# Attention and routed experts on one core: another order of work at the program's start and where the experts begin

## The chip, the cores and the metric

The kernel runs on one core of one Trainium2 chip. The metric is the device time of one execution in microseconds (us). Lower is better.

## The reference, cut to what matters

64 sequences of 128 tokens with 256 features go through cross attention with 16 heads, and then through a routed feed-forward layer of 8 experts of which each token takes two. All numbers are 32-bit floats.

```python
x = x + xattn(layernorm(x), ctx, ctx, Wq, bq, Wk, bk, Wv, bv, Wo, bo)
# Q = q @ Wq + bq, K = k @ Wk + bk, V = v @ Wv + bv, 16 heads of 16
# softmax(Q K^T / 4) V, then @ Wo + bo
x = x + ffn(layernorm(x), router, gating, up, down)
# probs = softmax(x @ router); top 2, their probs through a softmax again
# per chosen expert e: (silu(x @ gating[e]) * (x @ up[e])) @ down[e], weighted sum
```

## The kernel before

Each engine has a program of its own, written out by hand in one order, and the engines meet at semaphores: PE (TensorE) is the block from line 484, ACT (ScalarE) from 804, DVE (VectorE) from 990, POOL (GpSimd) from 380, and SP (SyncE) from 263, which issues most DMAs. No scheduler changes the order, so an instruction that waits holds everything behind it on its engine.

**The attention stage.** `run_stage_a` walks over 16 groups of 4 sequences. For sequence i, PE multiplies the first scores (`scores`, L551), the values of the next sequence (`values`), the attention product of the previous one (`attend`, L576) and a transpose of the row maxima (`swap_max`, L557), then a key or query product for the next group (`keys`, `queries`, 128x512 each), and the scores again with the maximum taken off (`scores_swapped`, L565). DVE takes the row maxima (`row_maxes`, L1028), and turns and divides the attention rows (`turn_att` L1041, `divide_by_sums`, `turn_attn` L1056). ACT makes the exponentials in three instructions, of one, one and two banks (`softmax_exp`, L867), and copies products out of the banks (`copy_piece` L855, `copy_values` L861, `copy_normed` L834). The heads of one sequence reach their places in `heads` through DMAs (`spread`, L286): two for keys, two for queries, each from the copied `kT` or `qT`. The program's start, ahead of the first sequence, is written out on its own: loads, the first layernorm, keys, queries and values of group 0. In it `bv` is multiplied by `Wo` on PE, DVE adds the product to `bo_sb`, and POOL needs that for `x_bo` (L427).

**The expert stage.** The chosen rows lie sorted by expert in DRAM (`sorted_x`), written by POOL with indirect DMAs (`write_rows`, L434). A unit is 256 rows of one expert. SP loads it (`load_unit`), DVE turns it (`turn_unit`, L1327) and reads its row weights (`read_rows_ends`), ACT copies the expert's matrices to `held` (`hold`, L878 and L879), PE makes `gate` and `up_` (16 records each in the trace) and `down_`, ACT the silu (L873), DVE the product (`fuse`, L1333). Unit n's `gate` comes ahead of unit n-1's `down_`. What is left of the last two groups, their residual, layernorm and routing, is put between the first units by `behind_tile(t)`, where t is twice the unit's number or one more.

**The seam.** Between the two stages PE has this order, with nothing of the experts ahead of the last `attend`:

```python
pe.wait_ge(s_n2Tc, (GROUPS - 1) * 2)
attend(last, att)
gate(0, 0, 2)
up_(0, 0, 2)
behind_tile(0)      # project(62)
behind_tile(1)      # project(63)
```

`gate` of unit 0 writes banks 0 and 1 and `up_` banks 2 and 3. The four are the banks from which the exponentials of sequence 63 are read. `held[1]` is the same memory as `probs`, and `xs` is the same as `xn`.

## Time and profile before

| | us |
|---|---|
| median of three runs | 1276.99 |
| the three runs | 1276.99, 1273.31, 1278.37 |
| the profiled execution, its own time | 1274.27 |
| its span, first to last instruction | 1272.5 |
| PE busy | 1221.5 |
| DVE, ACT, POOL busy | 645.8, 561.3, 424.4 |
| attention stage, to the last `scores_swapped` | to 533.1 |
| expert stage, from `gate` of unit 0 | from 539.5 |

Times in a timeline are from the span's start. PE is the engine's matmuls, PEld its weight loads. SPq, ACTq and POOLq are DMA issues and other work of those engines' sequencers. A timeline's row merges neighbouring instructions of one kind; its bracket is the engine's idle time before it and what ended that, by the trace's semaphore events. A 32-bit matmul is two records of PE, a transpose one.

### The profile page before, as it was taken

The numbers are of one execution on the slowest core, as the hardware profiler recorded it, in microseconds if no ns is written. First come the engines' busy times: TensorE is split into PE (matmuls) and PEld (weight loads), VectorE is DVE, ScalarE is ACT, GpSimd is POOL, SyncE is SP. The second block draws the span as 40 slices with busy tenths as digits, with TensorE's granted clock in tenths as the row PEclk, the third lists the DMA queues.
The fourth block names the chain that finished last, engine by engine and source line by source line (L and its number), as shares of the span: only waits on it lengthen the run. The fifth ranks groups of instructions, "written<-read, shape, count | busy, mean of one in ns | idle before, by whom it ended". The sixth has DMA issues, their size and how long they took to land.

```text
span 1272.5 us, 30742 instructions
## 1 busy us (share of the span) xinstructions
PE 1221.5 (96%) x11214; PEld 991.1 (78%) x11215; DVE 645.8 (51%) x1762; ACT 561.3 (44%) x924; POOL 424.4 (33%) x354
## 2 busy tenths in 40 slices
PE   6999999999999999799999999999999999999996
PEld 3677777777767676578887888888888888888996
DVE  3778888888888778623453222332222222232332
ACT  3566666666666665535322222222222322222442
POOL 3211333333333333322464222223332322222322
PEclk9999999999999999899999999999999999999999
DMA  4444455545545332424344333333333433333332
GB/s 130 138 117 122 152 152 149 157 151 154 155 140 151 114 117 82 106 48 67 77 89 71 50 50 50 53 52 53 50 50 50 54 50 52 51 50 43 53 51 33
DMA packets 171586, 112.44 MB, mean 88 GB/s; under 512 B 103345, under 2 KB 158641, under 8 KB 171473
## 3 DMA queue, kind: packets, MB, share of 16 engines
q1 hardware_dynamic: 143984, 72.75, 23.2%
q0 software_dynamic: 26400, 37.09, 16.6%
q8 instruction: 76, 1.25, 0.4%
q10 hardware_dynamic: 1088, 1.05, 0.3%
q14 instruction: 38, 0.30, 0.1%
HBM read 48.59 MB, written 45.46 MB: 74 GB/s over the span
## 4 chain that ended last, share of the span: by engine, by line
PE 89%; DVE 4%; DMA 2%; issue 2%; ACT 1%; SPq 0%; POOL 0%; another core or an unknown queue 0%; ACTq 0%; POOLq 0%; DVEq 0%
PE banks L522 71%; PE banks L551 5%; PE banks L565 4%; PE banks L576 4%; DVE row_max L1028 1%; PE banks L528 1%; PE banks L557 1%; DMA heads<-qT 1%; PE banks L592 1%; DMA out<-x_sb,token 1%; PE banks L600 1%; DVE att_rows L1041 1%; DVE q_less L1035 1%; DMA ctxT_sb<-in_ctx 0%; PE banks L606 0%
## 5 line engine op out<-in xcount | busy, mean ns | idle before, releaser
L481 POOL DMA_INDIRECT out<-x_sb,token x135 | 210.4, 1559 | 478.2 <-DVE x_sb L1346 413.5
L873 ACT ACTIVATE qT<-banks 128x1024 f32<-128x1024 f32 (+1 forms) x75 | 70.4, 939 | 488.6 <-PE banks L522 430.4
L1333 DVE TENSOR_TENSOR heads<-qT,banks 128x1024 f32<-128x1024 f32 (+1 forms) x75 | 83.5, 1113 | 356.7 <-PE banks L522 338.8
L522 PE MATMUL banks<-xnT,probs 128*128 128x256 f32 (+1 forms) x1184 | 242.7, 361 | 4.4 <-issue 4.4
L522 PE MATMUL banks<-down_sb,heads 128*128 x1080 | 245.5, 379 | 1.2 <-DVE x_sb L1346 0.9
L522 PE MATMUL banks<-xnT,kT 128*128 128x256 f32 (+1 forms) x1216 | 244.8, 359 | 0.0
L522 PEld LDWEIGHTS banks<-xnT,probs 128*128 128x128 f32 x1184 | 208.6, 191 | 32.9 <-issue 7.9
L522 PEld LDWEIGHTS banks<-xnT,kT 128*128 128x128 f32 x1216 | 213.1, 192 | 26.6 <-issue 1.0
L522 PEld LDWEIGHTS banks<-down_sb,heads 128*128 128x128 f32 x1080 | 204.0, 190 | 29.2 <-issue 2.2
L434 POOL DMA_INDIRECT sorted_x<-xn,slots_now x128 | 125.2, 978 | 251.5 <-PE banks L551 139.6
L1028 DVE TENSOR_REDUCE row_max<-banks 128x16 f32<-128x2048 f32 x64 | 146.6, 2291 | 64.2 <-PE banks L551 64.1
L867 ACT ACTIVATE probs<-banks 128x512 f32<-128x512 f32 (+1 forms) x192 | 128.1, 740 | 41.8 <-PE banks L565 40.5
L1346 DVE TENSOR_SCALAR x_sb<-banks,weight 128x256 f32<-128x256 f32 x135 | 59.8, 480 | 124.1 <-PE banks L522 115.7
L551 PE MATMUL banks<-heads 32*128 32x128 f32 x2048 | 75.0, 283 | 6.7 <-DMA heads<-qT 4.8
L576 PEld LDWEIGHTS banks<-probs,v_aug 128*32 128x32 f32 x2048 | 52.7, 110 | 31.9 <-issue 31.3
L565 PE MATMUL banks<-q_less,heads 32*128 32x128 f32 x2048 | 76.0, 285 | 1.1 <-DVE q_less L1035 1.1
L551 PEld LDWEIGHTS banks<-heads 32*128 32x128 f32 x2048 | 65.3, 189 | 12.9 <-issue 8.8
L576 PE MATMUL banks<-probs,v_aug 128*32 128x128 f32 x2048 | 70.0, 278 | 4.5 <-ACT probs L867 4.5
L522 PE MATMUL banks<-wo_sb,attnT 128*128 128x256 f32 x256 | 73.2, 409 | 0.7 <-DVE attnT L1056 0.7
L565 PEld LDWEIGHTS banks<-q_less,heads 32*128 32x128 f32 x2048 | 63.7, 188 | 11.7 <-issue 9.7
L522 PE MATMUL banks<-ctxT_sb,wk_sb 128*128 128x512 f32 x128 | 61.9, 608 | 8.3 <-DMA ctxT_sb<-in_ctx 7.8
L522 PE MATMUL banks<-wv_sb,ctxT_sb 128*128 128x256 f32 x256 | 66.0, 380 | 0.4 <-ACT probs L867 0.4
(165 smaller groups left out, 1269.2 us busy)
## 6 DMA issues: line engine op xcount, KB each, us to landing
xn<-sorted_x SPq DMA_DIRECT2D x240, 64.0 KB
x_sb<-in_x SPq DMA_DIRECT2D x16, 512.0 KB, 4.0
ctxT_sb<-in_ctx SPq DMA_DIRECT2D x16, 512.0 KB
heads<-kT SPq DMA_DIRECT2D x128, 64.0 KB
heads<-qT SPq DMA_DIRECT2D x128, 64.0 KB
out<-x SPq DMA_DIRECT2D x16, 512.0 KB
gate_sb<-_L_ffn_kernel_gating_EDF SPq DMA_DIRECT2D x8, 512.0 KB
up_sb<-in_L_ffn_kernel_up_EDF SPq DMA_DIRECT2D x8, 512.0 KB
```

Of the source, the lines that this page charges most:

```text
L434: pool.indirect_dma_start(out=sorted_x[:, :], out_offset=bass.IndirectOffsetOnAxis(ap=slots_now[:, g % 2, i:i + 1], axis=0), in_=xn2[:, g ...
L481: pool.indirect_dma_start(out=out[:, :], out_offset=bass.IndirectOffsetOnAxis(ap=token[:, v, h:h + 1], axis=0), in_=ys[:, 2 * u + h, :], i ...
L522: last = nc.tensor.matmul(dst, lhsT, rhs, start=(i == 0), stop=(i == len(pairs) - 1))
L528: last = nc.tensor.transpose(bank[:, b * P:(b + 1) * P], xn[:, b, c * P:(c + 1) * P], ident[:])
L551: last = nc.tensor.matmul(score_banks(i)[:, j, c * TOK:(c + 1) * TOK], q_heads[strip(j), i % 2, c, :], k_heads[strip(j), i % 2, c, :], sta ...
L565: last = nc.tensor.matmul(score_banks(i)[:, j, c * TOK:(c + 1) * TOK], k_heads[strip(j), i % 2, c, :], q_less[strip(j), c, :], start=True, ...
L576: last = nc.tensor.matmul(bank[32 * j:32 * j + 32, q * TOK:(q + 1) * TOK], v_aug[:, i % 3, 4 * q + j, :], probs[:, j, c, :], start=True, s ...
L867: nc.scalar.activation(probs[:, j:j + n].rearrange("p j h t -> p j (h t)"), score_banks(i)[:, j:j + n], ACT.Exp, scale=DK ** -0.5).then_in ...
L873: nc.scalar.activation(gatedT[:, 0:w * F], gate_up[:, 0:w * F], ACT.Silu).then_inc(s_silu, 1)
L1028: nc.vector.reduce_max(row_max[:].rearrange("p (j r a) -> p j r a", r=16, a=2)[:, :, 0:4, 1], score_banks(i).rearrange("p j (h t) -> p j h ...
L1333: nc.vector.tensor_tensor(fusedT[:, u, 0:w * F], gatedT[:, 0:w * F], gate_up[:, 1024:1024 + w * F], ALU.mult).then_inc(s_fuse, 1)
L1346: last = nc.vector.tensor_scalar(ys[:, 2 * u + h, :], work[:, 0, h * D:(h + 1) * D], weight[:, v, h:h + 1], None, ALU.mult)
```

## The change

Six things are done, in the program's start and at the seam.

1. PE multiplies `ident` by itself 12 times into bank 6, ahead of the first keys.
2. `wo` and `wv` are loaded only once x has landed, the second context block once the first has.
3. The queries of group 0 are made in halves: of sequences 0 and 1 first (two products of 128x256, counted on two semaphores of their own), ahead of the product of `bv` with `Wo`, and of sequences 2 and 3 behind it, in banks that the keys have left. ACT copies the second half of the keys behind the two halves of the normed x instead of ahead of them. SP's `spread` of the first two sequences' queries waits for their two copies alone.
4. The first `scores` no longer waits for the copies of all queries and of the values; PE waits for those behind it.
5. At the seam `gate` of unit 0 stands ahead of the last `attend` and waits for the first two exponentials of sequence 63 alone; `project(62)` comes ahead of `up_`. DVE turns unit 0 and reads its weights ahead of `row_maxes(63)`; ACT does `hold(0, 0)` ahead of the square of x1 of sequence 61.
6. ACT copies the logits of group 14 behind unit 1 instead of behind `silu(2)`, and the second half of group 15's x1 ahead of `silu(5)` instead of behind it.

```diff
--- before.py
+++ after.py
@@ -203,6 +203,7 @@
...
         s_piece, s_piece_c = sem("keys_queries_product"), sem("keys_queries_ready")
+        s_first_q, s_first_qc = sem("first_two_queries_product"), sem("first_two_queries_ready")
         s_v, s_vc = sem("values_product"), sem("values_ready")
@@ -280,7 +281,10 @@
...
                 u, b = i // GROUP % 2, i % GROUP
-                wait(sp, s_piece_c, i // GROUP * 4 + 2 + 2 * o)
+                if o == 1 and i < 2:
+                    sp.wait_ge(s_first_qc, 2)
+                else:
+                    wait(sp, s_piece_c, i // GROUP * 4 + 2 + 2 * o)
                 wait(sp, s_scoreT, i - 1)
@@ -302,6 +306,7 @@
...
             sp.dma_start(bo_sb[:], bo.partition_broadcast(P)).then_inc(s_bo, 16)
+            sp.wait_ge(s_ctx[0], 16)
             load_ctx(1, 1)
@@ -623,8 +628,9 @@
...
                     wait(pe, s_x1, i - 2)
-                    wait(pe, s_vc, i + 1)
-                    wait(pe, s_piece_c, min(4 + i, SEQS))
+                    if i > 0:
+                        wait(pe, s_vc, i + 1)
+                        wait(pe, s_piece_c, min(4 + i, SEQS))
                     wait(pe, s_turn, i - 1)
@@ -648,6 +654,9 @@
...
                     wait(pe, s_exp, i * 3 - 1)
+                    if i == 0:
+                        pe.wait_ge(s_piece_c, 4)
+                        pe.wait_ge(s_vc, 1)
                     if b < 3:
@@ -693,19 +702,30 @@
...
             pe.wait_ge(s_masks, 1)
+            for _ in range(12):
+                nc.tensor.matmul(banks[:, 6, 0:P], ident[:], ident[:], start=True, stop=True)
             pe.wait_ge(s_wk, 16)
...
             norm_swapped(0, 1, work[:, 1, :])
+            def front_queries(m, half, bank, signal):
+                pe.wait_ge(s_xt1c, 2)
+                product(bank[:, 0:2 * TOK], [(wq_sb[:, c, m * P:(m + 1) * P], xnT[:, c, half * 2 * TOK:(half + 1) * 2 * TOK])
+                                             for c in range(DC)]).then_inc(signal, 1)
+
+            pe.wait_ge(s_wq, 16)
+            front_queries(0, 0, score[:, 2, :], s_first_q)
+            front_queries(1, 0, score[:, 3, :], s_first_q)
             pe.wait_ge(s_wo, 16)
...
             product(work[:, 0, 0:D], [(bv_rep[:, c, :], wo_sb[:, c, :]) for c in range(DC)]).then_inc(s_bvo, 1)
-            pe.wait_ge(s_wq, 16)
-            queries(0, 0, score[:, 2, :])
-            queries(0, 1, score[:, 3, :])
+            pe.wait_ge(s_piece_c, 2)
+            front_queries(0, 1, score[:, 0, :], s_piece)
+            front_queries(1, 1, score[:, 1, :], s_piece)
             pe.wait_ge(s_wv, 16)
-            values(0, 0, work[:, 1, :])
+            pe.wait_ge(s_first_qc, 1)
+            values(0, 0, score[:, 2, :])
             pe.wait_ge(s_const, 13)
@@ -774,10 +794,12 @@
...
             pe.wait_ge(s_n2Tc, (GROUPS - 1) * 2)
+            wait(pe, s_exp, SEQS * 3 - 1)
+            gate(0, 0, 2)
+            wait(pe, s_exp, SEQS * 3)
             attend(last, att)
-            gate(0, 0, 2)
+            behind_tile(0)
             up_(0, 0, 2)
-            behind_tile(0)
             behind_tile(1)
@@ -896,15 +918,15 @@
...
                         square_x1(i - 3)
-                    if two and b != 2:
-                        square_x1(i - 2)
-                    if b == 2 and prev:
-                        second_norm(g - 1, (2, 3))
                     if i == SEQS - 1:
...
                         hold(0, 0)
+                    if two and b != 2:
+                        square_x1(i - 2)
+                    if b == 2 and prev:
+                        second_norm(g - 1, (2, 3))
                     if nxt and b < 3:
@@ -924,18 +946,31 @@
...
 
-            for w_sb, w, signal in ((wk_sb, wk, s_wk), (wq_sb, wq, s_wq), (wo_sb, wo, s_wo), (wv_sb, wv, s_wv)):
+            def load_matrix(w_sb, w, signal):
                 act.dma_start(w_sb[:], w.rearrange("(c p) n -> p c n", p=P)).then_inc(signal, 16)
+
+            load_matrix(wk_sb, wk, s_wk)
+            load_matrix(wq_sb, wq, s_wq)
+            act.wait_ge(s_x, 16)
+            load_matrix(wo_sb, wo, s_wo)
+            load_matrix(wv_sb, wv, s_wv)
             first_norm(0, (0, 1, 2, 3))
...
             copy_piece(0, 0, 0, score[:, 0, :])
-            copy_piece(0, 0, 1, score[:, 1, :])
             copy_normed(0, 0, banks[:, 7])
             copy_normed(0, 1, work[:, 1, :])
-            copy_piece(0, 0, 2, score[:, 2, :])
-            copy_piece(0, 0, 3, score[:, 3, :])
+            copy_piece(0, 0, 1, score[:, 1, :])
+            def copy_front_queries(m, half, bank, ready, n, signal):
+                act.wait_ge(ready, n)
+                nc.scalar.activation(qT[:, 0, 2 * half:2 * half + 2, m, :], bank[:, 0:2 * TOK].rearrange("p (b t) -> p b t", t=TOK),
+                                     ACT.Identity, bias=bq_sb[:, m:m + 1]).then_inc(signal, 1)
+
+            copy_front_queries(0, 0, score[:, 2, :], s_first_q, 1, s_first_qc)
+            copy_front_queries(1, 0, score[:, 3, :], s_first_q, 2, s_first_qc)
+            copy_front_queries(0, 1, score[:, 0, :], s_piece, 3, s_piece_c)
+            copy_front_queries(1, 1, score[:, 1, :], s_piece, 4, s_piece_c)
             act.wait_ge(s_masks, 3)
-            copy_values(0, work[:, 1, :])
+            copy_values(0, score[:, 2, :])
             run_stage_a(stage_a)
@@ -943,7 +978,7 @@
...
                     square_x1(SEQS - 1)
-                if t == 4:
+                if t == 3:
                     copy_logitsT(GROUPS - 2, att)
@@ -951,8 +986,9 @@
...
                     gap_exp(GROUPS - 2)
-                if t in (9, 10):
-                    copy_x1T(GROUPS - 1, t - 9, work[:, 1, :])
+                if t == 9:
+                    copy_x1T(GROUPS - 1, 0, work[:, 1, :])
+                    copy_x1T(GROUPS - 1, 1, work[:, 1, :])
                 if t == 11:
@@ -1242,6 +1278,18 @@
...
 
+            def turn_unit(n, u, w, loads):
+                dve.wait_ge(s_xs[u], loads * 80)
+                nc.vector.transpose(xsT[:, u, 0:w * D], xs[:, u, 0:w * D].rearrange(
+                    "p (i c r) -> p c i r", i=w * STRIPS, c=DC)).then_inc(s_xtc, 1)
+
+            def read_rows_ends(n, u, v, w):
+                nc.vector.scalar_tensor_tensor(pair[:, 0:w], ends[:, u, 0:w, 2:4], tile_rank[:, bass.ds(n, 1)],
+                                               ends[:, u, 0:w, 0:2], ALU.is_equal, ALU.mult).then_inc(s_pair, 1)
+                nc.vector.tensor_copy(token[:, v, 0:w], ends[:, u, 0:w, 4])
+                dve.wait_ge(s_pair, n + 1)
+                nc.vector.reduce_sum(weight[:, v, 0:w], pair[:, 0:w], AX.X).then_inc(s_meta, 1)
+
             def stage_a(g, u, core, prev, prev2, prev3, nxt, far):
@@ -1252,6 +1300,10 @@
...
                         second_shift(g - 1)
+                    if i == SEQS - 1:
+                        dve.wait_ge(s_piece, GROUPS * 4)
+                        turn_unit(0, 0, 2, 1)
+                        read_rows_ends(0, 0, 0, 2)
                     row_maxes(i)
@@ -1322,23 +1374,11 @@
...
 
-            def turn_unit(n, u, w, loads):
-                dve.wait_ge(s_xs[u], loads * 80)
-                nc.vector.transpose(xsT[:, u, 0:w * D], xs[:, u, 0:w * D].rearrange(
-                    "p (i c r) -> p c i r", i=w * STRIPS, c=DC)).then_inc(s_xtc, 1)
-
             def fuse(n, u, w):
...
                                         ALU.mult).then_inc(s_fuse, 1)
-
-            def read_rows_ends(n, u, v, w):
-                nc.vector.scalar_tensor_tensor(pair[:, 0:w], ends[:, u, 0:w, 2:4], tile_rank[:, bass.ds(n, 1)],
-                                               ends[:, u, 0:w, 0:2], ALU.is_equal, ALU.mult).then_inc(s_pair, 1)
-                nc.vector.tensor_copy(token[:, v, 0:w], ends[:, u, 0:w, 4])
-                dve.wait_ge(s_pair, n + 1)
-                nc.vector.reduce_sum(weight[:, v, 0:w], pair[:, 0:w], AX.X).then_inc(s_meta, 1)
 
@@ -1386,9 +1426,6 @@
...
 
-            dve.wait_ge(s_piece, GROUPS * 4)
-            turn_unit(0, 0, 2, 1)
-            read_rows_ends(0, 0, 0, 2)
             turn_unit(1, 1, 2, 1)
```

PE's order from its first instruction to the first `scores` (`heads`), before and now; `wk_sb`, `wq_sb`, `wo_sb`, `wv_sb` are the four matrices, `att_rows` holds `bv` repeated. Rows that only continue the one ahead are left out.

```order
L522 MATMUL banks<-ctxT_sb,wk_sb 128x512 [waits ctx_loaded_0,wk_loaded,masks_ready]
L528 MATMUL banks<-ident,xn 128x128 [waits x_normed]
L522 MATMUL banks<-wo_sb,att_rows 128x256 [waits bv_repeated,wo_loaded]
L522 MATMUL banks<-xnT,wq_sb 128x512 [waits normedT_ready,wq_loaded]
L522 MATMUL banks<-wv_sb,ctxT_sb 128x256 [waits wv_loaded]
L551 MATMUL banks<-heads 128x128 [waits values_ready,keys_queries_ready,normedT_ready,key_heads_spread_0,bias_out_ready,query_heads_spread_0,masks_ready,consts_ready]
```

```order
L706 MATMUL banks<-ident 128x128 [waits masks_ready]
L706 MATMUL banks<-ident 128x128 x11
L527 MATMUL banks<-ctxT_sb,wk_sb 128x512 [waits ctx_loaded_0,wk_loaded]
L533 MATMUL banks<-ident,xn 128x128 [waits x_normed]
L527 MATMUL banks<-xnT,wq_sb 128x256 [waits normedT_ready,wq_loaded]
L527 MATMUL banks<-wo_sb,att_rows 128x256 [waits bv_repeated,wo_loaded]
L527 MATMUL banks<-xnT,wq_sb 128x256 [waits normedT_ready,keys_queries_ready]
L527 MATMUL banks<-wv_sb,ctxT_sb 128x256 [waits first_two_queries_ready,wv_loaded]
L556 MATMUL banks<-heads 128x128 [waits normedT_ready,key_heads_spread_0,bias_out_ready,query_heads_spread_0,masks_ready,consts_ready]
```

The product for the output bias moved behind the first half of the queries, and the first scores lost two waits.

PE's order at the seam, before and now; `xnT` is the turned unit, `kT` its expert's matrices, `probs` with `v_aug` the last attention product, `attnT` the projections of sequences 62 and 63.

```order
L565 MATMUL banks<-q_less,heads 128x128 x7
L576 MATMUL banks<-probs,v_aug 32x128 [waits probs_ready,values_ready,x1T_ready,att_turned,table_steps,experts_loaded]
L522 MATMUL banks<-xnT,kT 128x256 [waits weights_held,tileT_ready]
L522 MATMUL banks<-xnT,kT 128x256 [waits weights_held]
L522 MATMUL banks<-wo_sb,attnT 128x256 [waits attnT_ready]
L522 MATMUL banks<-wo_sb,attnT 128x256 [waits attnT_ready,att_turned]
```

```order
L570 MATMUL banks<-q_less,heads 128x128 x7
L527 MATMUL banks<-xnT,kT 128x256 [waits probs_ready,tileT_ready,x1T_ready,weights_held,table_steps,experts_loaded]
L581 MATMUL banks<-probs,v_aug 32x128 [waits values_ready,att_turned,probs_ready]
L527 MATMUL banks<-wo_sb,attnT 128x256 [waits attnT_ready]
L527 MATMUL banks<-xnT,kT 128x256 [waits weights_held]
L527 MATMUL banks<-wo_sb,attnT 128x256 [waits attnT_ready,att_turned]
```

The gate moved ahead of the last attention product, and the projection of sequence 62 moved between that and `up_`.

## Rows read from the trace of the kernel before

**Rows 1.** The page: chain that ended last, share of the span by engine.

```profile
PE 89%; DVE 4%; DMA 2%; issue 2%; ACT 1%; SPq 0%; POOL 0%; another core or an unknown queue 0%; ACTq 0%; POOLq 0%; DVEq 0%
```

**Rows 2.** PE's waits from 500 us on: total us, times, longest.

```profile
PE banks L576 <- ACT probs L867: 4.5, 1, 4.5
...
PE banks L600 <- ACT xn2T L838: 1.7, 1, 1.7
...
PE banks L606 <- ACT logitsT L842: 1.3, 1, 1.3
```

**Rows 3.** Timeline of the start: start us, us, engine, line, operation, count, idle before.

```profile
2.79 0.29 POOL L388 TENSOR_SCALAR_AFFINE_SELECT ident<-ident 128x128 f32<-128x128 f32 x1 [0.24 <-POOL v_aug L386]
...
7.80 5.33 PE L522 MATMUL banks<-ctxT_sb,wk_sb 128*128 128x512 f32 x8 [7.80 <-DMA ctxT_sb<-in_ctx]
...
9.34 2.08 ACT L810 ACTIVATE xn<-x_sb,shift,rstd 128x256 f32<-128x256 f32 x4 [4.74 <-DVE shift L1015]
...
12.97 1.04 PE L528 MATMUL banks<-ident,xn 128*128 128x128 f32 x8
```

**Rows 4.** The same timeline, from the copies to the first scores.

```profile
13.76 1.07 ACT L834 ACTIVATE xnT<-banks 128x512 f32<-128x512 f32 x2
...
13.96 2.44 SPq L286 DMA_DIRECT2D heads<-kT  x4
...
14.98 3.67 PE L522 MATMUL banks<-xnT,wq_sb 128*128 128x512 f32 x8
...
15.48 2.35 POOL L427 TENSOR_TENSOR x_bo<-x_sb,bo_sb 128x1024 f32<-128x1024 f32 x1 [6.38 <-DVE bo_sb L1320]
...
18.49 1.03 PE L522 MATMUL banks<-wv_sb,ctxT_sb 128*128 128x256 f32 x4
...
18.69 0.69 ACT L855 ACTIVATE qT<-banks,bq_sb 128x512 f32<-128x512 f32 x1 [1.03 <-PE banks L522]
19.40 2.38 SPq L286 DMA_DIRECT2D heads<-qT  x4
...
22.07 1.17 PE L551 MATMUL banks<-heads 32*128 32x128 f32 x32 [2.56 <-DMA heads<-qT]
```

**Rows 5.** Timeline of the seam, up to the last attention product.

```profile
527.85 2.29 DVE L1028 TENSOR_REDUCE row_max<-banks 128x16 f32<-128x2048 f32 x1 [1.30 <-PE banks L551]
...
531.96 1.17 PE L565 MATMUL banks<-q_less,heads 32*128 32x128 f32 x32
...
533.09 0.67 DVE L1327 STREAM_TRANSPOSE xnT<-xn 128x512 f32<-128x512 f32 x1
...
535.26 2.00 ACT L867 ACTIVATE probs<-banks 128x512 f32<-128x512 f32 x3 [1.31 <-remote]
...
537.62 1.93 PE L576 MATMUL banks<-probs,v_aug 128*32 128x128 f32 x32 [4.49 <-ACT probs L867]
```

**Rows 6.** Timeline of the seam, behind it.

```profile
539.48 9.21 PE L522 MATMUL banks<-xnT,kT 128*128 128x256 f32 x32
...
544.25 0.72 DVE L1041 STREAM_TRANSPOSE att_rows<-banks 128x512 f32<-128x512 f32 x1 [8.24 <-remote]
...
550.25 1.10 PE L522 MATMUL banks<-wo_sb,attnT 128*128 128x256 f32 x4 [0.70 <-DVE attnT L1056]
...
551.19 7.07 PE L522 MATMUL banks<-xnT,probs 128*128 128x256 f32 x32
```

**Rows 7.** POOL's timeline at the seam: first and last of 8 writes in a row.

```profile
537.11 0.97 POOL L434 DMA_INDIRECT sorted_x<-xn,slots_now  x1 [2.74 <-issue]
...
546.00 0.96 POOL L434 DMA_INDIRECT sorted_x<-xn,slots_now  x1 [0.31 <-issue]
```

**Rows 8.** Stretches: length; PE, PEld, DVE, ACT, POOL busy; granted clock; DMA share; GB/s.

```profile
536.80:543.60 6.80, 5.98 (x42) 4.82 (x43) 0.00 (x0) 1.74 (x2) 4.96 (x6) 0.50 0.63 143
...
663.90:673.30 9.40, 6.00 (x23) 3.90 (x22) 1.54 (x4) 0.89 (x1) 6.87 (x8) 1.00 0.40 117
673.30:676.80 3.50, 3.35 (x7) 2.03 (x7) 1.88 (x6) 1.83 (x2) 0.31 (x1) 0.51 0.39 91
```

## The prediction

> **What bounds the kernel now.** I read the page first: the chain of work that ended last is 89% PE [rows 1]. So a change counts only where PE waits or runs slowly, and the next view is the list of PE's waits, which also shows how few there are. From 500 us on three of them concern this change: 4.5 us ahead of the last attention product, 1.7 and 1.3 us for two of ACT's copies [rows 2]. The third view is the timeline of the start. PE's first work begins at 7.80 and the first scores at 22.07 [rows 3, 4]. There the reader is to see two things: that PE's first 8 records take 5.33 us where 8 of the same size take 3.67 later, and that the last link ahead of the scores is not PE but a row of eight head DMAs on SP, the last four from 19.40. The fourth view is the timeline of the seam with the granted clock by stretches [rows 5, 6, 8]. PE stands from 533.1 to 537.6, and from 536.80 to 543.60 the granted clock is 0.50, the 1.2 GHz level, after those 4.5 us of standing.
>
> **Start: idle products.** 12 products of `ident` are 24 records of 128 columns. They can start when `ident` is made, at 3.08 [rows 3]. Eight transposes of that size take 1.04 us, so 24 take 3.1 us at the fast pace and 6.2 at half of it: they end between 6.2 and 9.3, around the 7.80 at which the keys begin. They lie in time in which PE has nothing else. If PE is fast by then, the keys take 3.67 us instead of 5.33 and end at 11.5 instead of 13.1, and what is late next is the normed x, done at 9.34 + 2.08 = 11.42. The transposes then stand at 11.5 to 12.6 instead of 12.97 to 14.0. Bounds: nothing (the pace doesn't change, or a tail of idle products holds the keys) to these 1.5 us; I take 1.4.
>
> On this the Trainium skill, page "TensorE: Matmul & The Clock Gate", Part 1, says that how many of the first matmuls run slow differs from one run of the same kernel to another, which speaks against counting on these products. By it the start would be worth 1.5 us in some executions and 2.8 in others; the keys' slow records [rows 3] are of one execution only.
>
> **Start: order.** ACT from 11.5: first keys 0.69 (the duration of a copy of 128x512) [rows 4], both halves of the normed x 1.07, second keys 0.69. That ends at 14.0, so SP's four key DMAs start at 14.0 as before (13.96) and take 2.44, until 16.45. The first half of the queries starts on PE at 13.3 and takes 3.67 / 2 = 1.8; its two copies, at most 0.5 each, are done by 15.7, ahead of SP. So SP issues the first query heads at 16.45 instead of 19.40, which is 2.95 us earlier, and from that issue to the first scores it stays 22.07 - 19.40 = 2.67: scores at 19.1. Meanwhile PE does the bias product (0.9), the other half of the queries (1.8) and the values (1.03) [rows 4], until 18.9; that cover is 0.2 us short of being the bound itself. POOL's 2.35 us for `x_bo`, behind the bias product and DVE's sum, begin near 16.6 instead of 15.48 and end at 19.0 [rows 4], when SP has issued the last head DMA: the load of the next x, which waits for both, keeps its distance to the first scores. The two waits taken from the first scores cost nothing today and now would, since the values' copy ends at 19.4; where they stand now, behind the 1.17 us of scores, they are hidden again. The later loads (`wo`, `wv`, second context) bring operands that PE wants at 15.1, at 18.0 and behind the first scores, seven us and more after the context's arrival at 7.80; I cost them at nothing. Start in all: 1.5 (PE stays slow) to 3.1, taken 2.8. Behind it every wait is relative, so the gain stays.
>
> **Seam.** The exponentials begin at 535.26 and the first two of three, half of their 2.00 us, end at 536.3 [rows 5]. `gate` of unit 0 can start at 536.5 instead of the attention product at 537.62. From there PE does `gate` 3.5 (half of the 7.07) [rows 6], `attend` 1.1, `project(62)` 0.9, `up_` 3.5, `project(63)` 0.9: 9.9 us, so `gate` of unit 1 could start at 546.4 against 551.19. Of the old 13.6 us from 537.62, some 3 were the low clock. Against this stand two things.
> The first is the signal of `attend`. Its records end at 539.55, and DVE, which had nothing else, begins `turn_att` only at 544.25, 4.7 us later [rows 5, 6]. ACT's exponentials, too, begin 2.1 us behind the last record of the scores they need (533.13). Both fall into POOL's rows of indirect writes (eight from 537.11 to 546.97) [rows 7]. What holds the signals isn't shown; that they come late while POOL writes is. `attend` now ends at 541.1, inside the same writes (DVE reaches the routing of group 13 about 0.9 us earlier, since one turn of 0.67 and its small reads are gone ahead of it). With the same 4.7 us DVE turns at 545.8, its four operations take about 2 (an estimate from the 0.72 of the first), and `project(63)` runs from 547.8 to 548.7. So 2.4 us are left of the 4.8.
> The second is the clock: PE still stands 3.4 us, from 533.1 to 536.5. If the clock falls as it did, for 6.8 us, `up_` ends 3.4 us later, at 548.9, and 1.3 us are left. Without the held signals the seam gives the full 4.8, and 6.6 if the exponentials start when their scores are done. Bounds 1.0 to 6.6; I take 2.4, since the row on a signal in these writes is nearest.
> DVE's turn of unit 0 (0.67; with its small reads 1.0, an estimate) goes into the 1.30 us in which DVE waits ahead of `row_maxes(63)` [rows 5]; without that cover it would hold the maxima by up to 1.0. ACT's `hold` ahead of a square is done while PE works on sequence 63 and changes nothing behind it, as long as the signal for the exponentials is what comes late. DVE frees unit 0's buffer near 527.5 instead of 533.8, so SP issues the loads of unit 2 some 6 us earlier; the last head DMA is out by then (its scores ended before 527.85), so nothing stands behind them.
>
> **The two copies.** The logits' copy and the x1 copy now run while `gate` runs, so PE's waits of 1.3 and 1.7 go: 2.9 us. What is late next there is nothing: ACT does them in its idle time ahead of the silu.
>
> **Sum.** 2.8 + 2.4 + 2.9 = 8.1 us. From the profiled execution's own 1274.27 that gives 1266.2. This execution lies 2.7 below the median of 1276.99 and inside the three runs; the four times shown average 1275.7, from which the sum gives 1267.6, and this I forecast.
>
> **Rivals.**
> - *The seam opens fully* (the signals come in time): start 2.8, copies 2.9, seam 4.8 to 6.6, in all 10.5 to 12.3: about 1264.3. For it: once POOL's writes are over, signals and records agree. Against: the writes stay where they are. Chance 0.17.
> - *PE stays slow at the start*: 1.5 instead of 2.8, or the idle products end behind the context's arrival: in all 6.8, 1268.9. For it: they need up to 9.3 and the keys could go at 7.8. Chance 0.16.
> - *The seam gives nothing*: the wait moves from `attend` to `project(63)`, whose chain waits for a signal that comes only when POOL is done (547 or later), and the clock is low for longer. In all 5 to 6 us, 1270.2. For it: the late signals [rows 6, 7]. Chance 0.16.
> - *Slower than before.* In one other place PE runs into POOL's writes at full pace: from 663.90 to 676.80 it did 30 records in 12.9 us, which take 6.6 at 7.07 / 32, a loss of 6.3 [rows 8]. In the seam it was spared so far, perhaps because it was standing or at the low clock. If `gate`, `attend` and `up_` at full pace now bring that loss to the seam, the seam gives 0 and costs 6.3: 5.7 - 6.3, so 0.6 slower, 1276.3. The point from which it decides: gaps between PE's records as at 663.90 while POOL is still in its eight writes, which last 9.9 us. Chance 0.05.
> - *The change doesn't do what it says*: the orders printed show every move in place; that it is spoiled elsewhere is in the cases above.
>
> **Chances and range.** Forecast 0.46, rivals 0.17, 0.16, 0.16, 0.05. 0.5%, 6.4 us, is about what a measurement of this kernel can tell from no change. The forecast is 8.1 with about 2 us of scatter either way, so it is over 6.4 in eight cases of ten (0.37); the full seam adds 0.17, slow PE 0.09, the empty seam 0.03. That is 0.66 for faster, 0.30 for within 0.5%, 0.04 for slower. The range takes the full seam to 1262.0 and the empty one, from the highest run of before, to 1273.5.
>
> **What would show it.** In the changed profile: PE's 8 key records in about 3.7 us; the first `heads<-qT` issue near 16.5 and first scores near 19.1; xnT,kT of unit 0 starting near 536.5 - 2.8 = 533.7, and unit 1's `gate` 5.2 us earlier than 551.19, at 546.0; PE's waits L600 and L606 in the expert stage gone. It is wrong if the key records still take 5.3, if first scores stand above 20.5, if PE idles over 3 us between `up_` and `project(63)`, or if a new gap stands in units 1 to 12.

## The result and the profile after

The changed kernel takes 1269.42 us (median of 21 runs, 1266.72 to 1273.54), the kernel before 1276.98 in the same comparison (21 runs). The ratio is 0.9942, with an interval of 0.9933 to 0.9951: 7.4 us, or 0.58%, faster. The forecast was 1267.6. The span of the profiled execution went from 1272.5 to 1267.9, so this pair shows 4.6 of the 7.4 us. PE's share of the chain of waits went from 89% [rows 1] to 87%.

The start of the changed kernel, from its timeline (start us, us, engine, line, operation; idle before and what ended it); the line numbers are those of the changed kernel:

```profile
3.12 4.63 PE L706 MATMUL banks<-ident 128*128 128x128 f32 x24 [3.12 <-POOL ident L393]
...
8.00 3.67 PE L527 MATMUL banks<-ctxT_sb,wk_sb 128*128 128x512 f32 x8 [0.26 <-DMA ctxT_sb<-in_ctx]
...
9.59 2.07 ACT L832 ACTIVATE xn<-x_sb,shift,rstd 128x256 f32<-128x256 f32 x4 [1.32 <-DVE shift L1051]
...
11.72 1.09 PE L533 MATMUL banks<-ident,xn 128*128 128x128 f32 x8
...
14.17 2.44 SPq L290 DMA_DIRECT2D heads<-kT  x4
...
16.66 2.51 SPq L290 DMA_DIRECT2D heads<-qT  x4
17.08 2.35 POOL L432 TENSOR_TENSOR x_bo<-x_sb,bo_sb 128x1024 f32<-128x1024 f32 x1 [7.72 <-DVE bo_sb L1372]
...
19.47 1.17 PE L556 MATMUL banks<-heads 32*128 32x128 f32 x32 [0.41 <-DMA heads<-qT]
```

These rows answer to [rows 3, 4]. The idle products end at 7.75, before the context arrives. The keys take 3.67 us (before 5.33), the transposes begin at 11.72 (12.97), SP issues the first query heads at 16.66 (19.40), and the first scores stand at 19.47 (22.07): 2.60 us earlier. The keys end at 11.67 and ACT's norm at 11.66, so the transposes wait for both; the prediction had the norm last, at 11.42. `x_bo` ends at 19.43, and the next x load is issued at 19.51, when SP is through with the heads.

The seam, from three timelines of the same kernel, PE's, ACT's with DVE's, and POOL's:

```profile
529.42 1.17 PE L570 MATMUL banks<-q_less,heads 32*128 32x128 f32 x32
534.16 3.69 PE L527 MATMUL banks<-xnT,kT 128*128 128x256 f32 x16 [3.56 <-ACT probs L889]
537.78 1.08 PE L581 MATMUL banks<-probs,v_aug 128*32 128x128 f32 x32
...
539.76 3.62 PE L527 MATMUL banks<-xnT,kT 128*128 128x256 f32 x16
547.31 2.04 PE L527 MATMUL banks<-wo_sb,attnT 128*128 128x256 f32 x4 [3.94 <-DVE attnT L1092]
549.15 4.13 PE L527 MATMUL banks<-xnT,probs 128*128 128x256 f32 x10
```

```profile
532.71 2.00 ACT L889 ACTIVATE probs<-banks 128x512 f32<-128x512 f32 x3 [2.59 <-remote]
...
537.89 1.02 ACT L895 ACTIVATE qT<-banks 128x1024 f32<-128x1024 f32 x1 [1.87 <-issue]
...
545.23 0.72 DVE L1077 STREAM_TRANSPOSE att_rows<-banks 128x512 f32<-128x512 f32 x1 [12.45 <-remote]
```

```profile
533.88 0.97 POOL L439 DMA_INDIRECT sorted_x<-xn,slots_now  x1 [2.04 <-issue]
...
542.73 0.96 POOL L439 DMA_INDIRECT sorted_x<-xn,slots_now  x1 [0.30 <-issue]
```

Against [rows 5, 6, 7]: `gate` of unit 0 begins at 534.16, but the attention product ends at 538.86 and DVE begins to turn it only at 545.23, 6.4 us later; in the profile before it was 4.7. POOL's eight writes end at 543.69. Not every signal in this row of writes is late: ACT's silu, the line at 537.89, starts 0.04 us behind the recorded end of `gate` (537.85), one product before the attend. PE has finished `up_` at 543.37 and stands 3.94 us for `attnT` ahead of `project(63)`. Then the clock is low:

```profile
core 0: us, PE busy (x) PEld busy (x) DVE busy (x) ACT busy (x) POOL busy (x), PEclk, DMA share, GB/s
...
545.98:552.81 6.83, 5.50 (x13) 4.40 (x14) 3.63 (x9) 1.90 (x2) 0.00 (x0) 0.50 0.00 0
657.00:674.00 17.00, 12.77 (x54) 9.50 (x53) 5.44 (x20) 5.49 (x6) 10.65 (x11) 1.00 0.41 94
```

The columns are length, the busy time of PE, its weight loads, DVE, ACT and POOL, the granted clock, the share of the DMA engines and GB/s. In the second stretch the clock is full and PE is busy for only 12.77 of 17 us, like 663.90 to 673.30 in [rows 8]. From the end of `scores_swapped(63)` to `gate` of unit 1 the kernel before took 18.1 us (533.13 to 551.19), the changed one 18.6 (530.59 to 549.15). PE's waits from 500 us on, in total us, times, longest:

```profile
PE banks L527 <- issue: 5.5, 11, 1.3
...
PE banks L527 <- DVE attnT L1092: 3.9, 1, 3.9
PE banks L527 <- ACT probs L889: 3.6, 1, 3.6
```

The waits for the copies of `xn2T` and `logitsT`, 1.7 and 1.3 us in [rows 2], are gone from this list. "issue" is time in which PE waited for nothing that the profile shows; its 5.5 us (4.7 in the kernel before) lie in the expert stage, where POOL issues long rows of indirect writes.

### The profile page after: what moved, and what is told of

The parts are those of the page before. It is cut to its first block, busy times and chain, and to the rows that moved or that the text cites. A ratio compares the mean times of both kernels' runs of the same rounds, so it can differ in the third digit from the quotient of the medians.

```text
span 1267.9 us, 30811 instructions
## 1 busy us (share of the span) xinstructions
PE 1221.0 (96%) x11246; PEld 994.7 (78%) x11247; DVE 646.1 (51%) x1762; ACT 562.0 (44%) x926; POOL 423.9 (33%) x354
## 4 chain that ended last, share of the span: by engine, by line
PE 87%; DVE 5%; DMA 2%; issue 2%; another core or an unknown queue 2%; ACT 1%; SPq 0%; POOL 0%; ACTq 0%; POOLq 0%; DVEq 0%
PE banks L527 69%; PE banks L556 5%; PE banks L570 5%; PE banks L581 4%; DVE row_max L1064 1%; PE banks L562 1%; PE banks L533 1%; DMA heads<-qT 1%; PE banks L597 1%; DMA out<-x_sb,token 1%; PE banks L605 1%; DVE att_rows L1077 1%; DVE q_less L1071 1%; DMA x_sb<-in_x 0%
## 5 line engine op out<-in xcount | busy, mean ns | idle before, releaser
L570 PEld LDWEIGHTS banks<-q_less,heads 32*128 32x128 f32 x2048 | 63.7, 188 | 11.4 <-issue 9.5
L1071 DVE TENSOR_TENSOR q_less<-heads,banks 128x256 f32<-128x256 f32 x128 | 48.2, 418 | 30.7 <-PE banks L611 17.0
```

The costliest lines, as they stand in the source:

```text
L570: last = nc.tensor.matmul(score_banks(i)[:, j, c * TOK:(c + 1) * TOK], k_heads[strip(j), i % 2, c, :], q_less[strip(j), c, :], start=True, ...
L1071: nc.vector.tensor_tensor(q_less[:, c:c + 2, :], q_heads[:, i % 2, c:c + 2, :], bank[:, 0:TOK].unsqueeze(1).broadcast_to([P, 2, TOK]), ALU ...
```

## Experiments

Five groups of kernels ran, each group on one chip with the kernel before beside it. The kernel before took 1261.17 and 1260.57 us in the first two groups and 1279.01, 1279.08 and 1277.18 in the last three. In the profiles of the first two DVE and ACT begin at once when PE is done; in the profiles of the last three, as in those of before and after above, they begin late in places. I call the chips prompt and late for this. Each chip was used for one group only, so the runs can't tell a property of a chip from one of that occasion. Times are compared as ratios to the kernel before of the same group; the prices below are ratios times that kernel's time. Kernels of different groups are compared through these ratios, which is weaker than a comparison on one chip.

### The parts one by one (prompt chips)

The first group undid parts of the change. In e1 the seam and the copies are as before; in e2 the seam alone:

```diff
-            wait(pe, s_exp, SEQS * 3 - 1)
-            gate(0, 0, 2)
             wait(pe, s_exp, SEQS * 3)
...
-            behind_tile(0)
+            gate(0, 0, 2)
...
+            behind_tile(0)
```

> The changed kernel with its seam and its two copies put back as before, so only the start is changed. Theory (start worth 2.6 us at the first scores in the trace of after, and kept to the end): 2.4 to 3.2 us faster than before, 1273.8 to 1274.6. Rival (the gain of the start is lost again in the groups behind it, by waits on the query heads' DMA or by the clock): under 1 us, 1276 to 1277.5. Rival (the start also shifts the clock's low stretches for good): over 4 us, under 1273.

> The changed kernel with the seam alone put back (attend ahead of the gate, the row turn at its old place, ScalarE's order as before). Theory (the changed seam gives nothing or costs: in the profile of after PE waits 3.9 us for attnT in front of project(63) and the clock is at 0.50 from 545.98 to 552.81): as fast as the changed kernel or up to 2 us faster, 1267.5 to 1270. Rival (the seam gives the 2.4 us that the prediction put down): 1.5 to 3 us slower than the changed kernel, 1271 to 1272.5. Rival (the seam opens fully in executions without a profile): 4 to 5 us slower, 1273.5 to 1274.5.

e8 undoes the copies alone (`if t == 3` back to `if t == 4`, and `copy_x1T` again in tiles 9 and 10), and ran in the second group with e5, the changed kernel, and e6, the kernel before:

> The changed kernel with the two copies of xn2T and logitsT put back behind the second sequence's probabilities. Theory (they ended the waits of 1.7 and 1.3 us ahead of L600 and L606 on PE's path, 2.9 us in all): 2.4 to 3.2 us slower than the changed kernel. Rival (the waits only move to the next one, the score's bank or the row transposes): under 1 us slower.

> The changed kernel itself, on the chip of its neighbours in this group. In the runs so far the signals of TensorE came at once (attend ahead of the gate: att_rows 0.05 us behind the attend's end), while in the profiles of before and after they came 4.7 and 6.3 us late. Theory (the late signals belong to the executions or the chip, and not to the changed order): where they come at once, att_rows starts within 1 us of the attend, PE's wait ahead of project(63) is under 1 us, and the kernel is 10 to 12 us faster than before; where they come late, 7 to 8 us faster, as in the first runs. Rival (the changed order brings the late signals about): att_rows 4 us or more behind the attend in any case, 7 to 8 us faster.

> The kernel before once more, for a profile beside the others of this group. Theory (late signals of TensorE come with GpSimd's row writes issued back to back, and only on some chips or in some executions): either none is late in any of the group's kernels (exponentials 0.2 us behind the scores in front of the last attend, att_rows at once) or this kernel shows lags of 2 and 4.7 us as the first profile did. Time within 0.3% of the before of the comparison.

| kernel | median us | before us | ratio (95%) |
|---|---|---|---|
| e1 start alone | 1256.94 | 1261.17 | 0.9968 (0.9956 to 0.9979) |
| e2 without the seam | 1253.70 | 1261.17 | 0.9944 (0.9928 to 0.9960) |
| e8 without the copies | 1253.43 | 1260.57 | 0.9941 (0.9928 to 0.9955) |
| e5 changed | 1249.92 | 1260.57 | 0.9915 (0.9902 to 0.9929) |
| e6 before | 1261.19 | 1260.57 | 0.9998 (0.9988 to 1.0009) |

On a prompt chip the change is worth 10.7 us: the start 4.0 (e1), the copies 3.3 (0.9941 - 0.9915) and the seam 3.7 (0.9944 - 0.9915), in all 11.0. So the three parts add up within their intervals, which are 1 to 2 us wide either way. e1's 4.0 (2.6 to 5.5 by its interval) is above its theory's 2.4 to 3.2 and at the edge of the rival's "over 4", so the run does not decide between them. The theory of e2, that the seam gives nothing, falls there; 3.7 lies between its two rivals. e8's 3.3 is its theory's size, and e5's 10.7 its theory's 10 to 12. In e6 no signal at the seam is late: the exponentials start 0.07 us behind the scores and `att_rows` 0.04 behind the attend. e5's timeline of PE at the seam:

```profile
525.10 1.17 PE L570 MATMUL banks<-q_less,heads 32*128 32x128 f32 x32
527.79 3.69 PE L527 MATMUL banks<-xnT,kT 128*128 128x256 f32 x16 [1.51 <-ACT probs L889]
531.41 1.08 PE L581 MATMUL banks<-probs,v_aug 128*32 128x128 f32 x32
...
533.39 3.62 PE L527 MATMUL banks<-xnT,kT 128*128 128x256 f32 x16
536.84 1.03 PE L527 MATMUL banks<-wo_sb,attnT 128*128 128x256 f32 x4
537.71 7.07 PE L527 MATMUL banks<-xnT,probs 128*128 128x256 f32 x32
```

PE waits 1.51 us ahead of `gate`, then goes without a gap from there to `gate` of unit 1: 11.4 us from the end of the scores at 526.27, where e6, the kernel before on this chip, takes 14.8 (534.25 to 549.04). DVE and POOL in e5:

```profile
529.34 0.97 POOL L439 DMA_INDIRECT sorted_x<-xn,slots_now  x1 [1.41 <-issue]
...
532.56 0.72 DVE L1077 STREAM_TRANSPOSE att_rows<-banks 128x512 f32<-128x512 f32 x1 [4.32 <-PE banks L581]
```

`att_rows` starts 0.07 us behind the attend's end (531.41 + 1.08), inside POOL's same eight back-to-back writes, which begin at 529.34 and end at 539.16. So the writes alone don't hold the signal, nor does the changed order; it takes a late chip as well.

e6 also shows a way in which the start can give more than 2.6. Its first scores:

```profile
22.43 2.09 PE L551 MATMUL banks<-heads 32*128 32x128 f32 x32 [2.56 <-DMA heads<-qT]
```

The scores take 2.09 us, where they took 1.17 in [rows 4], and the values 2.08 instead of 1.03: behind its wait of 2.56 us PE went on at the low level, 1.2 GHz. In e1 the wait there is 0.41 us and the scores take 1.17. The first `scores_swapped` begin 5.0 us earlier in e1 than in e6 (24.80 against 29.82), 2.9 us earlier than in the first profile of before (27.71). These are single executions, on different chips; how often the kernel before starts in the slow way the runs don't tell.

### What the order at the seam does (prompt chip)

e4, in the first group, is the changed kernel with only the two products exchanged:

```diff
-            wait(pe, s_exp, SEQS * 3 - 1)
-            gate(0, 0, 2)
             wait(pe, s_exp, SEQS * 3)
             attend(SEQS - 1, ...)
+            gate(0, 0, 2)
```

> The changed kernel, but the last attend stands ahead of the first gate again, while the row turn on VectorE and ScalarE's order stay as changed. Theory (what PE's order does at the seam is to move a wait: for the probabilities ahead of the attend, 4.5 us in before, or for attnT ahead of project(63), 3.9 us in after): within 1 us of the changed kernel, and PE waits 4 to 4.6 us ahead of the attend and under 1.5 us ahead of project(63). Rival (the order is what gains at the seam): 2 to 5 us slower than the changed kernel, 1271.5 to 1274.5.

Measured 1251.77, ratio 0.9928 (0.9910 to 0.9945), between e2's 0.9944 and e5's 0.9915. PE waits 2.43 us for the probabilities ahead of the attend and none ahead of `project(63)`; the way from the scores to `gate` of unit 1 takes 13.8 us against 11.4 in e5 and 15.6 in e2. So here the exchange of the products is worth about 2 us and the moved turn with ACT's order the rest; by the trace 2.4 and 1.7, by the ratios 1.6 and 2.0, with intervals that overlap. The theory, that the exchange only moves a wait, is wrong in these traces, where the wait ahead of the attend is 2.43 us and the one that it should replace, ahead of `project(63)`, is absent in e5 too. The time alone, 1.6 us, would not decide it.

### POOL's writes later, and spread

e3, e7 and e10 are one kernel: the changed one with a wait in POOL's queue, so that the eight writes of group 13 begin when the last attention has been turned.

```diff
             def behind_tile(t):
                 if t == 0:
                     write_rows(GROUPS - 4, (6, 7))
+                if t == 0:
+                    pool.wait_ge(s_turn, SEQS)
                 if t in (0, 1):
                     write_rows(GROUPS - 3, range(GROUP * t, GROUP * t + GROUP))
```

> The changed kernel, but GpSimd begins its eight row writes of the last-but-one group of the first part only when VectorE has turned the last attention, so that none is issued while PE runs the gate, the last attend and the up product. Theory (PE's signal that the attend is done is held back while GpSimd issues its row writes: att_rows began 6.3 us behind the attend's end in after, 4.7 us in before): att_rows starts within 1 us of the attend's end, the 3.9 us wait in front of project(63) is gone, the clock doesn't fall there, and the time is 3 to 6 us under the changed kernel's, 1263.5 to 1266.5. Rival (the signal is late for a reason of PE's own, such as its queue of the up product): att_rows is as late as before, the time within 1 us of the changed kernel's, or later by what the held writes cost behind it.

> The kernel of the late row writes again, beside the changed kernel. Theory (the writes issued during the gate, the attend and the up product hold something at the seam, at the least the weights and rows behind them in the queues): 2 to 4 us faster than the changed kernel of this group. Rival (what it won over the kernel without the seam, 4.3 us, is all the changed seam's own): within 1 us of the changed kernel.

> The kernel of the late row writes a third time, for the case that this chip's before takes 1277 us, as the first profiles did, and not 1261. Theory (where TensorE's signals come late, they do so while GpSimd issues its writes back to back): on such a chip att_rows starts within 1 us of the attend's end, no wait ahead of project(63), and the kernel is 10 to 12 us faster than before instead of the changed kernel's 7.6. Rival (they are late whatever GpSimd does): lag and time as the changed kernel's, 7 to 8 us faster than before. On a chip whose before takes 1261 us it repeats the run before, 10 to 12 us faster, and says nothing on this.

On the prompt chips it took 1249.38 us, ratio 0.9908 (0.9890 to 0.9925), and 1250.36, ratio 0.9919 (0.9905 to 0.9932), beside e5's 0.9915: no difference, so e7's theory is wrong and its rival right. e3's question, whether the writes hold the signal, could not be answered there, since nothing is late on such a chip. On a late chip it took 1270.10 us, ratio 0.9920 (0.9900 to 0.9939), where the changed kernel had 0.9942 on another: 10.2 us faster than before, and e10's theory said 10 to 12. The intervals overlap, so the 2.8 us are not certain, but the trace answers the question. First the seam of e10:

```profile
536.20 2.00 ACT L891 ACTIVATE probs<-banks 128x512 f32<-128x512 f32 x3 [2.74 <-remote]
...
544.26 0.72 DVE L1079 STREAM_TRANSPOSE att_rows<-banks 128x512 f32<-128x512 f32 x1 [8.37 <-PE banks L583]
```

```profile
532.76 1.17 PE L572 MATMUL banks<-q_less,heads 32*128 32x128 f32 x32
537.81 5.38 PE L529 MATMUL banks<-xnT,kT 128*128 128x256 f32 x16 [3.88 <-ACT probs L891]
543.12 1.08 PE L583 MATMUL banks<-probs,v_aug 128*32 128x128 f32 x32
...
549.41 3.83 PE L529 MATMUL banks<-xnT,probs 128*128 128x256 f32 x17
```

`att_rows` now starts 0.06 us behind the attend's end (544.20), and no wait is left ahead of `project(63)`: scores to `gate` of unit 1 in 15.5 us instead of 18.6. The exponentials are still late, 2.3 us behind the scores' end at 533.93; ahead of them stand three back-to-back writes that this edit left alone, the last from 534.28 to 535.24. In all four late profiles with these three writes the exponentials start 0.8 to 1.0 us behind the end of the last of them (before 0.90, after 0.87, e9 0.78, e10 0.96). In e9 below, on the same chip with the writes where the changed kernel has them, `att_rows` was 3.4 us late, and ACT's silu, one product earlier in the same row of writes, 0.04. The kernel of e10 shows PE creeping in the expert stage:

```profile
655.55 3.83 PE L529 MATMUL banks<-down_sb,heads 128*128 x16
660.69 0.45 PE L529 MATMUL banks<-xnT,probs 128*128 128x256 f32 x1 [1.30 <-issue]
661.50 0.38 PE L529 MATMUL banks<-xnT,probs 128*128 128x256 f32 x1 [0.36 <-issue]
662.23 0.38 PE L529 MATMUL banks<-xnT,probs 128*128 128x256 f32 x1 [0.35 <-issue]
...
670.19 3.69 PE L529 MATMUL banks<-xnT,probs 128*128 128x256 f32 x16 [0.70 <-issue]
```

Each single record of 0.38 us stands behind an "issue" gap of 0.2 to 1.3 us. POOL in this stretch goes from 640.15 to 667.98 through 20 indirect DMAs with 0.30 us between them. PE's "issue" waits from 560 us on come to 7.3 us in 12 places; in e5, with the same rows of writes on a prompt chip, there is none. e11 therefore spreads the bursts behind the seam:

```diff
                 if t == 0:
-                    write_rows(GROUPS - 4, (6, 7))
                     pool.wait_ge(s_turn, SEQS)
-                if t in (0, 1):
-                    write_rows(GROUPS - 3, range(GROUP * t, GROUP * t + GROUP))
+                    write_rows(GROUPS - 4, (6, 7))
+                if t < 4:
+                    write_rows(GROUPS - 3, (2 * t, 2 * t + 1))
...
-                if t in (10, 11):
-                    write_rows(GROUPS - 2, range(GROUP * (t - 10), GROUP * (t - 9)))
-                if t in (16, 17):
-                    write_rows(GROUPS - 1, range(GROUP * (t - 16), GROUP * (t - 15)))
-                if t in (18, 19):
-                    write_pads(t - 18)
+                if t in SPREAD_ROWS:
+                    write_rows(*SPREAD_ROWS[t])
+                if t in SPREAD_PADS:
+                    write_pads(SPREAD_PADS[t])
```

`SPREAD_ROWS` gives group 14's writes to tiles 10 to 15 and group 15's to tiles 16 to 20, one or two each; `SPREAD_PADS` gives the eight pad writes to tiles 21 to 25.

> The kernel of the late row writes, but GpSimd's bursts behind the seam are spread as well: of each group's eight row writes (and of the eight pad writes) one to four stand in one unit, between tiles 10 and 25, and the two writes of the group before and four of the eight at the seam wait for the last turned attention too. Theory (where TensorE's signals come late and PE creeps through its products with 'issue' gaps, it is while GpSimd issues eight to ten indirect DMAs back to back: 5 us of PE's time near 620 and 9 us near 657 to 670 in the run before on such a chip): on a chip whose before takes 1277 us or more the gaps of PE go below 2 us in all and the kernel is 16 to 24 us faster than before, near what the changed kernel takes on the other chips. Where before takes 1261 us: no lag to remove, within 1.5 us of the changed kernel, 9 to 12 us faster than before. Rival (the creeping is the chip's own in that stretch of the program, whatever GpSimd issues): 9 to 11 us faster than before on either chip.

Measured on a late chip 1259.04 us against 1279.08, ratio 0.9845 (0.9825 to 0.9866): 20 us faster than before, and by the ratios 12 us faster than the changed kernel is on such a chip. PE's waits from 500 us on:

```profile
PE banks L567 <- DVE row_max L1069: 3.9, 2, 2.3
PE banks L602 <- DVE q_less L1076: 2.1, 2, 1.2
PE banks L532 <- ACT probs L894: 1.5, 1, 1.5
...
PE banks L561 <- issue: 0.4, 1, 0.4
```

The "issue" gaps of the expert stage are gone, the exponentials start 0.07 us behind the scores, and from the scores to `gate` of unit 1 it is 11.4 us, as in e5 on its prompt chip. From the first `down_` to the last e11 takes 687.5 us (551.49 to 1238.95), the same as e5 (544.61 to 1232.07); in the first profile of the changed kernel it was 695.5 (557.87 to 1253.33). The rival, 9 to 11 us, falls. The edit moves the issuing of the DMAs and their transfers together, so which of the two makes PE creep is not separated. Whether spreading costs or gains anything on a prompt chip was not run.

e12 adds one more edit: in each group of attention the two back-to-back writes of the second sequence are taken apart.

```diff
                         if b == 1:
-                            write_rows(g - 3, (0, 1))
+                            write_rows(g - 3, (0,))
+                        if b == 2:
+                            write_rows(g - 3, (2,))
...
                         if b == 1:
-                            write_rows(g - 3, (2,))
+                            write_rows(g - 3, (1,))
```

> The spread kernel, and in each group of attention GpSimd's two row writes that stood back to back in the second sequence are taken apart: one in the second and one in the third sequence, so that no two follow each other there. Theory (on chips with late signals two back-to-back writes suffice to hold TensorE's signals 0.5 to 1.1 us, once in each group of the trace of the spread kernel; the waits that follow and the clock's falls behind them make that chip some 6 us slower by the last scores than the others): where before takes 1277 us or more, 1 to 5 us faster than the spread kernel (which was 20 us faster than before). Where before takes 1261 us, within 1.5 us of the changed kernel's 10.7 us. Rival (a lag of 1 us is covered by PE's other work): as the spread kernel within 1 us.

A miss: 1265.62 us against 1277.18 on a late chip, ratio 0.9893 (0.9872 to 0.9915), about 6 us slower than e11. Its trace in the third sequence of a group (POOL's and PE's timeline, and DVE's first row behind the swap):

```profile
488.51 2.35 POOL L432 TENSOR_TENSOR x_bo<-x_sb,bo_sb 128x1024 f32<-128x1024 f32 x1 [1.74 <-PE banks L563]
491.04 1.03 POOL L439 DMA_INDIRECT sorted_x<-xn,slots_now  x1 [0.17 <-issue]
493.18 0.97 POOL L439 DMA_INDIRECT sorted_x<-xn,slots_now  x1 [1.11 <-PE banks L588]
```

```profile
491.19 0.33 PE L569 MATMUL banks<-ident,row_max 128*128 128x128 f32 x1
```

```profile
492.49 0.75 DVE L1078 TENSOR_TENSOR q_less<-heads,banks 128x256 f32<-128x256 f32 x2 [0.89 <-PE banks L569]
```

POOL does `keep_x`, 2.35 us, and 0.17 us behind it the moved write. PE's `swap_max` ends at 491.52, DVE takes it up at 492.49, 0.97 late. That DVE chain leads to `att_rows` and on to PE, and over the attention stage PE waits for it 11 times:

```profile
PE banks L534 <- DVE att_rows L1084: 5.1, 11, 0.7
```

In e11 this wait stood once, at 0.4 us. There the two writes of the second sequence went with a lag of the same DVE step too, 0.7 to 1.0 us in each of 12 groups, and PE did not wait for it; on e5's prompt chip, with the same two writes, no group has a lag of even 0.5. In e12 the lag in the third sequence is 1.0 to 1.2 us in each of 12 groups. So it moved from a place where PE's other work covers it to one where it does not, and PE's waits for it, 5.1 us, are near the 6 by which e12 is slower. It also shows that one write can be enough for a lag of 1 us. It is not always: the next one, from 493.18 to 494.15, stands alone as well, and ACT takes up PE's transposes 0.04 us behind their end (493.96), inside it.

### The idle products

e9 is the changed kernel without its 12 products of `ident`:

```diff
-            for _ in range(12):
-                nc.tensor.matmul(banks[:, 6, 0:P], ident[:], ident[:], start=True, stop=True)
```

> The changed kernel without its 12 idle products on ident, all else as changed. Theory (the products bring the clock up before the keys: eight keys 3.67 us instead of 5.33, and transposes and key product start earlier; the prediction's 1.4 us out of the start's whole gain, which came out at 4.2 us in the run of the start alone): the first keys take 5.3 us again and the kernel is 1.2 to 1.8 us slower than the changed one, so 8.9 to 9.5 us faster than before where signals are prompt (before 1261), 5.6 to 6.2 where they are late (before 1277). Rival (the order of the loads and of the query heads carries all of the start's gain): within 0.5 us of the changed kernel. Rival (the products carry most of it): 3 us or more slower than the changed kernel.

On a late chip it took 1275.08 us, ratio 0.9968 (0.9950 to 0.9985), where the changed kernel had 0.9942 on another: 3.3 us, and from 1.0 to 5.5 by e9's own interval alone.

```profile
7.86 5.16 PE L527 MATMUL banks<-ctxT_sb,wk_sb 128*128 128x512 f32 x8 [7.86 <-DMA ctxT_sb<-in_ctx]
...
20.55 1.17 PE L556 MATMUL banks<-heads 32*128 32x128 f32 x32 [0.42 <-DMA heads<-qT]
```

The keys take 5.16 us again, the transposes begin at 12.85 instead of 11.72, and the first scores stand 1.08 us later than in the first profile of the changed kernel, 1.4 later than in e5 (19.12). Against e10, on e9's own chip, it is only 0.64 (19.91), since there the idle products ran until 8.61 and the keys stood behind them: SP issued the second context, which waits for the first, at 7.55, but the keys began at 8.40. So by the traces the products are worth 0.6 to 1.4 us at the first scores, and twelve are too many in some executions. By time the 3.3 us fit the rival "3 us or more" as well as, at the interval's lower end, the theory's 1.2 to 1.8; the run does not decide it.

## Why the prediction came out right, and where it did not

The number held, 7.4 us against 8.1. The time itself, 1269.42, is nearer to the rival "the seam gives nothing" (1270.2) than to the forecast 1267.6, and the traces say the same of the mechanism. The terms held in part.

- **Idle products, 1.4.** Right where the context's arrival bounds the keys. They ended at 7.75, inside the forecast 6.2 to 9.3, the keys took 3.67, and e9 has the first scores 1.1 to 1.4 us later than after and e5. Too high where the products' own end bounds them: 0.6 against e10. The page "TensorE: Matmul & The Clock Gate" of the Trainium skill, Part 1, says that how many of the first matmuls run slow differs between runs of one kernel. In the eleven profiled executions with these products the 24 records took between 4.29 and 5.49 us, which fits it, and the keys behind them 3.60 to 3.97; so what varied fell mostly on the idle products, and the first scores stood at 19.1 to 19.9.
- **Start in all, 2.8.** Right in the first pair of profiles (2.60 at the first scores; query heads at 16.66 against a forecast 16.45). Too small against e6: the wait ahead of the first scores can leave PE at the low level for the scores and values behind it, and then the start is worth 5.0 us by the trace. The runs of e1 say 4.0 (2.6 to 5.5). I had the row for it, 2.56 us of standing at 22.07 [rows 4], and costed only the wait. By e1's median the term was too small by about 1.2 us, if e1's chip stands for the first one; by its interval it may have been right.
- **Later loads, 0.** Consistent: PE has no new wait for `wo`, `wv` or the second context. It was not tried alone.
- **Seam, 2.4.** Wrong on the chip it was forecast for. The step that failed is "with the same 4.7 us DVE turns at 545.8", and project(63) at 547.8. With the start's 2.6 taken off, the forecast was attend's end at 538.5, DVE at 543.2 and `project(63)` at 545.2; they came at 538.86, 545.23 and 547.31. The lag taken as fixed was not: 4.7 us in before, 2.7 us ahead of the end of POOL's row, and 6.4 in after, 1.5 us behind it. So the wait moved to `project(63)`, 3.94 us, the clock fell behind it and ran at 0.50 through most of `gate` of unit 1, and the seam cost 0.5 us up to the start of that `gate` and 2.3 us up to the first `down_` (558.10 against 557.87, where 2.54 had been gained by `scores_swapped(63)`). That is the rival "the seam gives nothing", for which 0.16 was given, in this profile, and the prediction's own sign of being wrong, over 3 us idle between `up_` and `project(63)`. On prompt chips the other rival came true: the seam opened fully, at the pace of 9.9 us that was forecast, plus a wait of 1.51.
- **Two copies, 2.9.** Right: both waits are gone, and e8 gives 3.3 us; e8's own waits for them are 1.7 and 1.3 again.
- **Slower rival.** PE did not creep in the seam. It creeps late in POOL's longest rows of DMAs, as at 663.90 in [rows 8].

With the seam at nothing the parts measured on prompt chips give 4.0 + 3.3 + 0 = 7.3, against the measured 7.4; with the 2.3 us that the seam cost in the late profile they give 5.0. In that pair of profiles 2.6 us are gained at the first scores, 0.2 are left at the first `down_`, and 4.4 come behind it, where the two copies stand for 2.9. The start, the seam and the copies were not taken apart on a late chip, so how the 7.4 divides there stays open. That the total came out near 8.1 with the seam wrong by 2.4 us or more is in part luck: gains elsewhere, above their forecast, stood against its loss.

## What to carry to other kernels

A wait that ends with a signal should be costed by what holds the signal: here from nothing up to the end of GpSimd's row of indirect writes and 1.8 us more (e9), not by the lag once seen. Where a profile shows an engine starting microseconds behind the record that it waits for ("<-remote"), or PE creeping behind "issue", look at what GpSimd issues at that moment and spread it; on a late chip that was worth more (12 us) than the whole change, and on a prompt one it was not run. And price a wait of PE with the slow records behind it.

## What the runs showed of the hardware

- On late chips some of TensorE's signals reach the others late while GpSimd issues indirect DMAs in a row: 4.7 us (before), 6.4 (after), 3.4 (e9); with the writes moved away 0.06 (e10), and 0.07 for the exponentials of e11. Others in the same rows are prompt: 0.04 us for ACT's silu in after and in e9. On prompt chips the same rows of writes do nothing (0.07 us in e5). The kernel before is 16 to 19 us slower on late chips and the changed one 19.5 (1269.42 against 1249.92); e11 takes back some 12 of these. What distinguishes the chips, and which signals of a row are held, the runs don't tell.
- The Trainium skill, page "Perfetto Trace Analysis", section "Tensor Engine Instruction", says that the profiler computes a matmul's end from its size, and that the semaphore update follows when PSUM has acknowledged. So a late signal could be a late end. The prompt profiles agree with the modelled ends to 0.1 us. On late chips the next products are recorded at full pace while the attend's signal is missing (`up_` in 3.62 us), which speaks for a held signal; the records cannot prove it.
- In a long row of such DMAs PE itself creeps: 20 in a row in e10, and 7.3 us of "issue" gaps; none in e11, where at most six follow each other. Whether it is instructions or signals that arrive late there stays open.
- The first products behind a wait of 2.56 us ran at full pace in one execution (1.17 us, [rows 4]) and at half of it in another (2.09, e6) of the same kernel; the granted clock is 1.00 from 22.00 to 26.00 in the former, and 0.70 from 19.90 to 25.00 in the latter.

```profile
core 0: us, PE busy (x) PEld busy (x) DVE busy (x) ACT busy (x) POOL busy (x), PEclk, DMA share, GB/s
19.90:25.00 5.10, 2.57 (x33) 2.33 (x34) 0.35 (x1) 0.38 (x1) 0.00 (x0) 0.70 0.44 102
```
